# Beginning attention image by image: normalisation, projections, splits and transfers in smaller pieces

## The reference

```python
t = _to_tokens(x)
t = t + _L2_attn_ref(_ln_t(t), L2_attn_w_qkv, L2_attn_w_proj, L2_attn_b_proj)
t = t + _L2_ffn_ref(_ln_t(t), ...)
t = t + _L3_attn_ref(_ln_t(t), ...)      # causal
t = t + _L3_ffn_ref(_ln_t(t), ...)
```

## Time and profile before

| | |
|---|---|
| median of three runs | 1030.7 us |
| the profiled execution, whole | 1029.4 us |
| its span, first to last instruction | 1027.6 us |
| PE busy | 823.8 us (80%) |
| DVE busy | 447.6 us (44%) |
| ACT busy | 295.5 us (29%) |
| POOL busy | 233.5 us (23%) |
| mean granted TensorE clock | 0.878 |

### The profile page before, as it was taken

The page is one execution under the profiler, slowest core; times in us unless marked ns, Lnnn a source line. Parts: engine busy times, 40 slices in busy tenths (PEclk is TensorE's granted clock), DMA queues, the critical chain, the costliest instruction groups (busy, mean ns, idle before and its releaser), DMA issues. The chain is left out here.

```text
span 1027.6 us, 12446 instructions
## 1 busy us (share of the span) xinstructions
PE 823.8 (80%) x3900; PEld 520.7 (51%) x3901; DVE 447.6 (44%) x1129; ACT 295.5 (29%) x446; POOL 233.5 (23%) x314
## 2 busy tenths in 40 slices
PE   3769379899677786399999187775399999999993
PEld 2758236435544454166666144554256666666662
DVE  4974631698656543522222546554511212121213
ACT  3223135532234562022121133453012121212121
POOL 1150000573201100234443112340211221122110
PEclk8579678999888997599999688898599999999997
DMA  3000070000135602033111425952103006600003
GB/s 109 1 1 1 1 256 1 0 1 0 48 97 167 150 22 90 16 102 108 41 46 41 145 72 157 240 150 72 34 16 144 21 26 270 265 20 26 26 15 133
DMA packets 53617, 80.35 MB, mean 78 GB/s; under 512 B 10020, under 2 KB 45988, under 8 KB 50372
## 3 DMA queue, kind: packets, MB, share of 16 engines
q1 hardware_dynamic: 48040, 67.37, 20.9%
q0 software_dynamic: 5536, 12.46, 4.0%
HBM read 55.82 MB, written 11.27 MB: 65 GB/s over the span
## 5 line engine op out<-in xcount | busy, mean ns | idle before, releaser
L2030 PE MATMUL psum<-ring,f_x_t 128*128 x552 | 254.3, 604 | 1.3 <-DVE f_x_t L1898 1.3
L1891 DVE TENSOR_TENSOR f_gated<-f_silu,psum 128x512 f32<-128x512 f32 x69 | 47.4, 688 | 271.2 <-PE psum L2030 271.2
L2030 PEld LDWEIGHTS psum<-ring,f_x_t 128*128 128x128 f32 x552 | 101.6, 194 | 104.5 <-issue 104.4
L2044 PE MATMUL psum<-ring,f_gated_t 128*128 x552 | 130.7, 380 | 1.8 <-ACT f_gated_t L1957 1.8
L2044 PEld LDWEIGHTS psum<-ring,f_gated_t 128*128 128x128 f32 x552 | 101.2, 190 | 23.4 <-issue 12.7
L1957 ACT ACTIVATE f_gated_t<-psum 128x512 f32<-128x512 f32 x69 | 41.2, 597 | 237.1 <-PE psum L2037 237.1
L1953 ACT ACTIVATE f_silu<-psum 128x512 f32<-128x512 f32 x69 | 41.2, 597 | 113.7 <-PE psum L2030 113.7
L1478 PE MATMUL psum<-a_stack_k,a_stack_q 96*128 96x256 bf16 (+1 forms) x256 | 45.3, 289 | 25.3 <-DMA a_stack_k<-a_parts 14.2
L1758 POOL COPY f_from_now<-f_from_row 128x1 uint32 (+1 forms) x48 | 9.0, 188 | 206.8 <-PE psum L2023 203.3
L1761 POOL DMA_INDIRECT f_xs<-rows_in,f_from_now x48 | 47.5, 989 | 36.5 <-POOL f_from_now L1758 36.5
L1770 POOL DMA_INDIRECT rows_out<-f_y,f_to_now x46 | 46.1, 1001 | 36.4 <-POOL f_to_now L1767 35.3
(11 more groups left out here) (294 smaller groups left out, 1208.1 us busy)
## 6 DMA issues: line engine op xcount, KB each, us to landing
ring<-in_f_experts SPq DMA_DIRECT2D x24, 1536.0 KB, 7.7
a_stack_q<-a_parts SPq DMA_DIRECT2D x96, 64.0 KB, 2.8
a_stack_k<-a_parts SPq DMA_DIRECT2D x96, 64.0 KB, 2.7
rows_in<-h SPq DMA_DIRECT2D x4, 1024.0 KB, 5.8
ring<-rows_out SPq DMA_DIRECT2D x8, 512.0 KB, 5.4
a_wqkv<-in_a_wqkv SPq DMA_DIRECT2D x2, 768.0 KB, 4.4
x_in<-in_x SPq DMA_DIRECT2D x1, 1024.0 KB, 5.5
out<-x SPq DMA_DIRECT2D x4, 256.0 KB, 2.1
```

The source lines that it names most:

```text
L1891: dve.tensor_tensor(gated[:, b, :], silu[:, b, :], psum[:, 2 * b + 1, :], ALU.mult).then_inc(s_g, 1)
L2030: last = pe.matmul(psum[:, 2 * b + side, :], x_t[:, xb, t, :], k.ring[:, bass.ds(at + start, CHUNK)], start=(t == 0), stop=(t == CT - 1))
L2044: last = pe.matmul(psum[:, Y_BANK, 0:C], gated_t[:, b, P * a:P * a + P], k.ring[:, bass.ds(at + start, C)], start=(c == 0 and a == 0), sto ...
```

## The change

- `LayerNorm` works in pairs of tiles, an image at a time: statistics of image 0; then for each image the statistics of the next and the normalised tiles of this one. The four square roots stand at the head of ScalarE's list. All four blocks that normalise use it.
- In attention, turned images go into PSUM banks 4 to 7, and ScalarE alone copies them to `h_t`. q and k are computed for 512 tokens at a time: 8 projections `i`, 0 to 3 for images 0 and 1 and 4 to 7 for images 2 and 3. Their PSUM banks are 0, 1, 2, 3 and then 2, 3, 2, 3. Splits are 512 wide.
- Images 2 and 3 are turned between projections 1 and 2. Projection 4 stands ahead of the first scores; projections 5, 6 and 7 stand after heads 0, 2 and 4, and their splits between the maxima. The last four tiles of values move from after heads 1, 4, 8 and 10 to after heads 6, 7, 8 and 10.
- SyncE issues the transfers of the first stacks group by group, and `s_first` has a semaphore for each of the four groups.

The core of the diff:

```diff
+    def image_by_image(self, dve, t, out):
+        self.statistics(dve, t, 0)
+        for i in range(TT // 2):
+            if i + 1 < TT // 2:
+                self.statistics(dve, t, i + 1)
+            self.normalise(dve, t, out, i)
...
     def deviation(self, act):
-        act.wait_ge(self.s_moments, 2)
-        act.activation(self.sd[:], self.var[:], ACT.Sqrt).then_inc(self.s_sd, 1)
+        for i in range(TT // 2):
+            act.wait_ge(self.s_moments, 2 * i + 2)
+            act.activation(self.sd[:, 2 * i:2 * i + 2], self.var[:, 2 * i:2 * i + 2], ACT.Sqrt).then_inc(self.s_sd, 1)
...
-VALUES_AFTER = (1, 4, GROUP, GROUP + 2)
+VALUES_AFTER = (GROUP - 2, GROUP - 1, GROUP, GROUP + 2)
+SPLITS = 2 * 2 * CT
+SPLITS_BEFORE = SPLITS // 2 + 1
+SPLITS_AFTER = (0, 2, 4)
+def split_bank(i):
+    return i if i < SPLITS // 2 else 2 + i % 2
...
+            for g in range(SLOTS_G):
+                b, t = image_and_half(g)
+                for which in range(2):
+                    for part, done in enumerate((s_hi, s_mid, s_lo)):
+                        sp.wait_ge(done, 2 * t + which + 1)
+                        for c, combo in enumerate(COMBOS):
+                            if combo[which] == part:
+                                sp.dma_start((stack_q, stack_k)[which][HD * c:HD * c + HD, g],
+                                             parts[:, t, which, part, N * b:N * b + N]).then_inc(s_first[g], 16)
+            sp.wait_ge(s_lo, SPLITS)
...
             # VectorE
+            for i in range(SPLITS_BEFORE):
+                take_rest(i)
+                take_low(i)
...
             for i in range(FIRST_MAXIMA):
                 take_max(i)
+                if i in SPLITS_AFTER:
+                    take_rest(SPLITS_BEFORE + SPLITS_AFTER.index(i))
+                if i - 1 in SPLITS_AFTER:
+                    take_low(SPLITS_BEFORE + SPLITS_AFTER.index(i - 1))
...
             # ScalarE
+            take_turned(0)
+            take_turned(1)
+            split(0)
+            split(1)
+            take_turned(2)
+            take_turned(3)
+            split(2)
+            split(3)
+            take_values(0)
+            take_values(1)
+            for i in range(SPLITS // 2, SPLITS):
+                split(i)
...
             negate(0)
-            take_values(TT // 2 - 1)
+            for i in range(TT // 4, TT // 2):
+                take_values(i)
...
             # TensorE
+            def project_part(i):
+                half, t_out, which = i // (2 * CT), i // 2 % CT, i % 2
+                column = C * which + P * t_out
+                if i >= 4:
+                    pe.wait_ge(s_r, i - 1)
+                for t in range(CT):
+                    last = pe.matmul(psum[:, split_bank(i), :], wqkv[:, t, column:column + P],
+                                     h_t[:, t, BANK * half:BANK * half + BANK], start=(t == 0), stop=(t == CT - 1))
                 last.then_inc(s_qk, 1)
...
+            turn_image(0)
+            turn_image(1)
+            pe.wait_ge(s_w, 16 * WEIGHTS)
+            pe.wait_ge(s_hto, 2)
+            project_part(0)
+            project_part(1)
+            turn_image(2)
+            turn_image(3)
+            project_part(2)
+            project_part(3)
             for T in range(TT // 2):
                 project_values(T)
-            pe.wait_ge(s_r, 2 * CT)
+            pe.wait_ge(s_hto, 4)
+            for i in range(SPLITS // 2, SPLITS_BEFORE):
+                project_part(i)
+            pe.wait_ge(s_r, 2)
...
                 scores_for_max(i)
                 if i == GROUP - 1:
                     turn_maxima(0, GROUP)
+                if i in SPLITS_AFTER:
+                    project_part(SPLITS_BEFORE + SPLITS_AFTER.index(i))
                 if i in VALUES_AFTER:
                     project_values(TT // 2 + VALUES_AFTER.index(i))
+            pe.wait_ge(s_r, SPLITS)
```

More of the change, by code:

```diff
@@ L1074, in __init__, with statistics @@
         self.s_out = sem(f"{name}_out")
-    def statistics(self, dve, t):
-        for T in range(TT):
+    def statistics(self, dve, t, i):
+        for T in (2 * i, 2 * i + 1):
             dve.bn_stats(self.raw[:, T, :], t[:, T, :]).then_inc(self.s_raw, 1)
-        for T in range(TT):
+        for T in (2 * i, 2 * i + 1):
             dve.wait_ge(self.s_raw, T + 1)
@@ L1191, in attention @@
         s_vo = sm("v_out")
-        s_first = [sm("stacks_of_first_heads"), sm("stacks_of_last_heads")]
+        s_first = [sm(f"first_stacks_{i}") for i in range(SLOTS_G)]
         s_st = [sm(f"stack_loaded_{i}") for i in range(SLOTS_G)]
@@ L1216, in attention, with part_of @@
         QUADS = GROUP // 4
+        def part_of(i, part):
+            half, t, which = i // (2 * CT), i // 2 % CT, i % 2
+            return parts[:, t, which, part, BANK * half:BANK * half + BANK]
         def exponentials(i):
@@ L1292, in _, with take_rest, take_low @@
         def _(dve):
[L1293 to L1302, removed]
+            ln.image_by_image(dve, k.t, normed)
+            def take_rest(i):
                 dve.wait_ge(s_hi, i + 1)
-                dve.tensor_tensor(rest[:, i % 2, :], source, parts[:, t, which, 0, :], ALU.subtract).then_inc(s_r, 1)
+                dve.tensor_tensor(rest[:, i % 2, 0:BANK], psum[:, split_bank(i), :], part_of(i, 0), ALU.subtract).then_inc(s_r, 1)
+            def take_low(i):
                 dve.wait_ge(s_mid, i + 1)
-                dve.tensor_tensor(parts[:, t, which, 2, :], rest[:, i % 2, :], parts[:, t, which, 1, :],
-                                  ALU.subtract).then_inc(s_lo, 1)
+                dve.tensor_tensor(part_of(i, 2), rest[:, i % 2, 0:BANK], part_of(i, 1), ALU.subtract).then_inc(s_lo, 1)
+            for i in range(SPLITS_BEFORE):
+                take_rest(i)
+                take_low(i)
             def take_max(i):
@@ L1368, in _, with take_turned, split @@
             ln.deviation(act)
-            for i in range(0, TT // 2, 2):
+            def take_turned(i):
                 act.wait_ge(s_ht, i + 1)
[L1371 to L1375, removed]
+                act.activation(h_t[:, :, N * i:N * i + N], psum[:, 4 + i, :].rearrange("p (t n) -> p t n", t=CT),
+                               ACT.Copy).then_inc(s_hto, 1)
+            def split(i):
                 act.wait_ge(s_qk, i + 1)
-                act.activation(parts[:, t, which, 0, :], source, ACT.Copy).then_inc(s_hi, 1)
+                act.activation(part_of(i, 0), psum[:, split_bank(i), :], ACT.Copy).then_inc(s_hi, 1)
                 act.wait_ge(s_r, i + 1)
-                act.activation(parts[:, t, which, 1, :], rest[:, i % 2, :], ACT.Copy).then_inc(s_mid, 1)
+                act.activation(part_of(i, 1), rest[:, i % 2, 0:BANK], ACT.Copy).then_inc(s_mid, 1)
             def take_values(i):
@@ L1425, in _, with turn_image @@
         def _(pe):
-            for i in range(TT // 2):
+            def turn_image(i):
                 pe.wait_ge(ln.s_out, 2 * i + 2)
```

46 lines of the change are left out of this document (12 added, 34 removed).

## The result

Twenty timed executions of each kernel on the same chips: before 1030.45 us in the median (1026.15 to 1037.16), changed 1024.71 (1020.92 to 1029.4). The ratio is 0.9941, its 95% interval 0.9927 to 0.9956: by the ratio 6.1 us faster (4.5 to 7.5), where 7.4 had been forecast; the medians themselves differ by 5.7. The profiled execution took 1024.63 us around a span of 1022.9.

A forecast was written before the change was run, and what follows sets the result against it. The prediction took a chain of waits through six successive stages, ending in the last expert stage, to bound the kernel. First attention -6.3, second -3.5, experts +2.4 gave -7.4 us: 1023.3 us, range 1019.0 to 1029.0.

The forecast's parts named there:

- Normalisation: Attention opening, S being the start of its first statistics: first projection at S+7.4, only 0.8 us earlier than before.
- TensorE's queue up to the first scores: First attention's opening: TensorE's own queue ends last, first scores at S+23.0 against S+31.4, 8.4 us earlier.
- From the first scores to the loop: First attention: VectorE sets the pace, first maximum S+25.8, eighth S+35.4, loop S+41.1 against S+47.6; -6.3 us with signals.
- first rival: Attention openings: the clock falls late in the stretch before the loop, 1.5 to 3 us each, about 1027.5; chance 0.13.
- third rival: Attention openings: clock falls at the first scores, three projections at half clock; loop S+47.8, +6.1 us, 1036.8; chance 0.07.
- Second attention: Second attention's opening: loop at S+40.8 against S+44.3, -3.5 us, less because its stretch was already shorter.
- Experts: Expert layers: gate starts 0.6 us later, its 32 products at half clock take 32/6 = 5.3 us; +1.2 per layer, +2.4.
- Loops: Attention loops: SyncE's next stack waits for TensorE, 8.9 us longest, so it moves with the loop; no added time counted.
- loops longer by what the openings lose: Attention loops: a sign that would show the forecast wrong, the loops lengthening by what the openings lose.
- 1.00 in S+13 to S+40: Attention openings: a sign of the forecast, the granted clock staying at 1.00 from S+13 to S+40.
- 2, SyncE's queue: Attention openings: the loop goes by the end of SyncE's 48 transfers, so only -1.4 us, 1029.3; chance 0.09.
- 4, better than forecast: Openings and experts: warm-up early and no loss in the expert layers, -7.2 - 4.4 + 1.0, 1020.1 us; chance 0.09.

The follow-up runs named there:

- experiment 4: Changed kernel with the statistics of all 8 tiles at once in the attentions and the expert layers: 1017.81 us, ratio 0.9882.
- experiment 6: Changed kernel with the first stacks' 48 transfers in the old order, by part for two images at a time: 1037.45 us, ratio 1.0058.
- experiment 5: Changed kernel with all 8 projections and their splits ahead of the first scores, none between the maxima: 1030.25 us, ratio 0.9993.
- experiment 10: Changed kernel with SyncE's first expert prefetch in each attention waiting for the second group's rows of maxima: 1026.78 us, ratio 0.9975.
- experiment 12: Changed kernel with all expert prefetches of the attentions issued after SyncE's loop, behind its last stacks: 1022.21 us, ratio 0.9896.
- experiment 1: Changed kernel with the statistics of all 8 tiles at once in the expert layers alone: 1021.13 us, ratio 0.9904.
- experiment 3: Changed kernel with four unread products after each of the first three turned images in the expert layers: 1023.16 us, ratio 0.991.
- experiment 2: Kernel before with only the expert layers' statistics taken image by image: 1035.71 us, ratio 1.0031.
- experiment 7: Changed kernel with two unread products on TensorE ahead of each attention loop's first wait for rows of maxima: 1026.18 us, ratio 0.9957.
- experiment 11: Changed kernel with whole statistics everywhere and each prefetch behind that turn's stacks and the next group's rows of maxima: 1015.09 us, ratio 0.9872.

## Why the prediction was right, and where its terms were off

**Normalisation: right.** First projection forecast at S+7.4, measured S+7.5, and for the reason given, ScalarE's fourth square root; experiment 4 shows that the edit could have been left out.

**TensorE's queue up to the first scores: right.** S+23.0 forecast, S+23.1 measured, 23.2 the second time. SyncE's queue starts at S+11.9 (forecast 11.7), and TensorE waits for no stack ahead of the first scores. Experiment 6 shows the mechanism: with the old order SyncE's queue is last again.

**From the first scores to the loop: right.** First maximum S+25.9 (25.8), the eighth turned at S+35.4 (35.4), loop at S+41.1 (41.1), 42.0 the second time, by the first rival. Experiment 5 shows that the saving hangs on the three products between the maxima, and at a price that the expectation, made from the same terms, did not give: 1.5 to 2.5 us an attention expected, 3.6 to 7.0 measured. It had no term for the clock that fell after the wait for VectorE; the prediction's third rival had described that fall.

**Second attention: mechanism right, term too small.** The forecast took the first attention's marks less 0.3, -3.5; measured -5.5 and, by the means, -5.3. The clock rose sooner (8 projection records in 5.25 us against 6.26), so the scores came at S+22.1, and the rows of maxima landed 4.7 us after the turning, not 5.7.

**Experts: mechanism right, size off.** "32/6 = 5.3" was the faulty figure: the 6 records of a window at half clock include those that reach into it from its neighbours. The product takes 0.218 us, 32 of them 6.97. With the later start of 0.5 us a layer costs 2.7 us where the gate before took 4.83, and less where that had lost the clock by itself; measured by ratios, 3.8 and 3.2 us for two layers, forecast 2.4.

**Loops: the step that failed.** "In the loop its next stack waits for TensorE ..., so it moves with the loop" took the order of SyncE's and POOL's transfers for fixed. It isn't: the start moved by 5 us, and what falls together moved too. In the kernel before, the second attention's first prefetch stands 5.2 us ahead of the rows of maxima, and TensorE doesn't wait for them:

```profile
628.95 9.25 SPq L1601 DMA_DIRECT2D ring<-in_f_experts  x2
...
634.17 1.04 POOL L1272 DMA_DIRECT2D a_stack_q<-a_negated  x2 [2.13 <-DVE a_negated L1326]
...
637.02 0.82 PE L1503 MATMUL psum<-a_stack_q,a_stack_k 98*128 98x256 bf16 x4
```

In the changed one it is issued 0.7 us ahead of them (623.81, 624.52; the row's x2 takes in the next prefetch, at 631.45), and TensorE gets them at 630.59, after 1.91 us of idle. Experiment 10 shows that moving this prefetch only moves the wait. In experiment 12, with all prefetches behind the loop's last stacks, the second loop is some 5 us shorter in its one profile; waits and half clock fell together there, and nothing parts the two.

In the first attention the clock differs too, in windows of the changed kernel:

```profile
280.00:282.00 2.00, 2.00 (x12) 1.31 (x11) 1.27 (x2) 0.86 (x2) 0.00 (x0) 1.00 0.39 98
...
308.00:310.00 2.00, 1.32 (x11) 0.97 (x12) 1.03 (x2) 1.24 (x2) 0.00 (x0) 1.00 0.41 104
310.00:312.00 2.00, 1.79 (x11) 0.75 (x10) 1.86 (x4) 1.02 (x1) 0.00 (x0) 0.61 0.42 106
312.00:314.00 2.00, 2.00 (x12) 0.84 (x14) 1.01 (x2) 0.23 (x1) 0.00 (x0) 0.50 0.86 246
...
324.00:326.00 2.00, 2.00 (x18) 1.57 (x16) 1.95 (x5) 1.13 (x2) 0.00 (x0) 0.98 1.06 356
```

It falls just after the loop's start, and 17.1 us of the loop are at half clock (windows of 1 us, twice what is missing to 1.00, summed), 13.7 in one piece and 3.4 near the end; in the profile of before it is 3.4, near the end. The changed kernel's loops and transfers are those of experiments 1, 3 and 4 as well, and those of before are experiment 2's. All eight profiles, in us:

| profile | first loop | at half clock | second loop | at half clock | wait for the rows of its second group |
|---|---|---|---|---|---|
| before | 80.0 | 3.4 | 78.5 | 13.7 | none |
| before, second profile | 78.6 | 7.5 | 81.3 | 20.5 | none |
| experiment 2 | 79.0 | 4.4 | 82.1 | 20.5 | none |
| changed | 82.4 | 17.1 | 82.1 | 20.5 | 1.91 |
| changed, second profile | 81.9 | 6.8 | 83.1 | 23.9 | 1.29 |
| experiment 1 | 78.0 | 0.0 | 82.6 | 23.9 | 1.16 |
| experiment 3 | 82.3 | 10.2 | 82.5 | 23.9 | 1.30 |
| experiment 4 | 78.5 | 3.4 | 82.1 | 23.9 | 1.54 |

The means differ by +1.4 in the first loop and +1.8 in the second. The wait at the second group belongs to the change: it is in all five profiles with the new opening, and in none of the three with the old. The first loop is a matter of the execution: the same instructions take 78.0 to 82.4 us, and among the five the long ones have 6.8 to 17.1 us at half clock, the short ones 3.4 or less (the kernel before has 7.5 beside a loop of 78.6). That the clock is the cause is not shown, since no run changed the clock and nothing else; experiment 7 gave no answer. And how much of +1.4 and +1.8 is the change stays open. One of the prediction's own signs of being wrong, loops longer by what the openings lose, came true in part.

**The rivals.** 1, the clock falling in the stretch ahead of the loop: it came, but small, in the first attention and not in every execution. In the first profile the clock is 1.00 up to 310.4; in the second it is 0.50 from 306.1 to 309.6, S+36.9 to S+40.4, windows of 1 us:

```profile
305.16:306.16 1.00, 0.87 (x5) 0.46 (x4) 0.41 (x1) 0.51 (x2) 0.00 (x0) 0.97 0.48 125
306.16:307.16 1.00, 1.00 (x4) 0.87 (x3) 0.51 (x1) 0.39 (x1) 0.94 (x2) 0.50 0.30 76
```

The profiles of experiments 1, 3, 4 and 12 have the same 3.4 us, and in these five the loop begins at S+41.9 to S+42.0; without a fall it begins at S+41.1, and at S+40.3 in experiments 10 and 11 (experiment 7 falls too, and with its filler begins at S+42.8). That is 0.8 to 1.7 us, where the rival had 1.5 to 3; the sign "1.00 in S+13 to S+40" failed there. 2, SyncE's queue: the queue ends at 311.2, when the loop has run for 3 us, and does not hold it; what it foresaw came back smaller, as the transfers' meeting in the loop. 3, projections at half clock between the maxima: not in the changed kernel (each four records in 1.88 us). Experiment 5 shows a fall in that place once the projections are away. Its sum has a slip: S+23 and 24.1 us are S+47.1, not S+47.8; with 0.48 us for a record of the values, which is what the earlier trace rows give, it is S+47.9. 4, better than forecast: the openings were, by 1.5 us, and the experts were not.

**Row and rule.** In the first profile the granted clock stayed 1.00 through an opening whose gaps were up to 1.6 us, and fell at 310.4, after pauses of 1.61 and 0.57 us, TensorE busy 1.32 and 1.79 of 2 us in the windows around; in the second it fell at 306.1, in the opening, after pauses of up to 1.59 us. The rule that I weighed (the Trainium skill, TensorE: Matmul & The Clock Gate, "HAM oscillation") names long idle gaps as what loses the clock; read as I read it, that without them the clock stays, it would have kept it. The trace does not agree with that reading.

**The sum.** -11.3 + 3.8 + 5.6 in the profiles, where the forecast had -9.8 + 2.4 + 0: the 1.3 us between 7.4 and 6.1 are what is left of errors on both sides, 1.5 us too little gain in the openings, 1.4 too little loss in the experts, and nothing at all for the loops. That the total came so near is in part luck.

## What to carry to other kernels

Where a long queue of small transfers feeds the first use, order it by the consumer, and then fill the consumer's waits with products it owes anyway: of the 11 us that both gave the openings here, the order alone gave 0 to 2, and the products alone cost 2 to 4. A piecewise start on one engine is worth only what the next engine can take up, and pieces of work that break another engine's run can cost it its clock. A change of a few us in a kernel whose executions differ by 8 to 11 us, as the twenty of each do here, needs more than one profile before a stage's share is believed. When an opening gets shorter, look at which large transfers now meet which small ones; a stage whose code is unchanged is not one whose time is.

## What the runs showed of the hardware

The gate's products of 8 columns keep TensorE 1.00 busy in every window and still run at a granted clock of 0.50 from first to last (0.218 us each; in experiment 1, behind unbroken transposes, 0.13 in the mean): TensorE was busy with them for 7 us, and the clock did not rise. And in the loop the clock stayed at 0.50 in 312:314 with TensorE busy for all of 2.00 us. A transfer of 4 KB (the rows of maxima) lands after 2.1 us in the median in experiment 12, with few large transfers beside it, after 2.6 in the kernel before and 3.9 in the changed one, and after up to 7.7.
